# A decoder stack on one core: causal mask added and maximum taken by one VectorE instruction in self attention, softmax row tile by row tile, normalisations in a pipeline

## What is computed

```python
x = x + _L0_attn_ref(_layernorm(x), ...)    # causal self attention, 16 heads, 4 key heads
x = x + _L0_xattn_ref(_layernorm(x), ...)   # each token picks 2 of its 4 sets
x = x + _L0_ffn_ref(_layernorm(x), ...)     # 16 experts, 4 per token
x = x + _L1_attn_ref(_layernorm(x), ...)    # gated delta rule, 16 heads
x = x + _L1_xattn_ref(_layernorm(x), ...)   # queries: x; keys: x and 64 context tokens
x = x + _L1_ffn_ref(_layernorm(x), ...)     # 128 experts, 48 kept, 8 per token
```

```python
def _layernorm(x, axis=-1, eps=1e-05):
    m = jnp.mean(x, axis=axis, keepdims=True)
    v = jnp.var(x, axis=axis, keepdims=True)
    return (x - m) / jnp.sqrt(v + eps)
...
    scores = jnp.einsum('bkgqd,bksd->bkgqs', qg, k) * scale
    causal = jnp.triu(jnp.full((S, S), -jnp.inf, dtype=x.dtype), k=1)
    scores = scores + causal
    attn = jax.nn.softmax(scores, axis=-1)
    out = jnp.einsum('bkgqs,bksd->bkgqd', attn, v)
```

## Time and profile before

| | us |
|---|---|
| median of 3 runs (4146.95 to 4150.4) | 4150.28 |
| the profiled execution | 4138.86 |
| its span, first to last instruction | 4137.1 |
| PE, DVE, ACT, POOL busy in it | 3579.5, 2639.7, 1644.6, 1412.7 |
| rotation of the keys on VectorE, start to end: self, cross | 0.74, 1.19 |
| `at_wo`'s transfer is issued; TensorE's first projection starts | 7.24; 27.20 |
| self attention, about | 26 to 675 |
| delta rule, about | 1151 to 2889 |
| cross attention, about | 2943 to 3870 |

### The profile page before, as it was taken

The page is one execution under the profiler, slowest core; times in us unless marked ns, Lnnn a source line. Parts: engine busy times, 40 slices in busy tenths (PEclk is TensorE's granted clock), DMA queues, the critical chain, the costliest instruction groups (busy, mean ns, idle before and its releaser), DMA issues. The chain is left out here.

```text
span 4137.1 us, 57933 instructions
## 1 busy us (share of the span) xinstructions
PE 3579.5 (87%) x17616; PEld 2756.4 (67%) x17616; DVE 2639.7 (64%) x7558; ACT 1644.6 (40%) x4218; POOL 1412.7 (34%) x2085
## 2 busy tenths in 40 slices
PE   7999997589678999999999999998499999999565
PEld 5676765445366888888888888886356556556454
DVE  5666565532247888888888888873666666666531
ACT  3444442133234455555554545441243443443221
POOL 0000000068615555555555555552111111111055
PEclk9999998589868999999999999999699999999665
DMA  2000002335500111111111111110100000000346
GB/s 75 0 0 0 0 0 68 116 65 85 117 14 19 40 28 40 29 36 30 35 37 27 37 27 39 28 21 12 57 1 0 0 0 0 0 0 0 115 111 144
DMA packets 220951, 149.99 MB, mean 36 GB/s; under 512 B 117104, under 2 KB 208656, under 8 KB 220208
## 3 DMA queue, kind: packets, MB, share of 16 engines
q1 hardware_dynamic: 193664, 111.49, 10.5%
q0 software_dynamic: 22848, 31.69, 4.6%
q10 hardware_dynamic: 4224, 4.19, 0.3%
HBM read 105.64 MB, written 41.61 MB: 36 GB/s over the span
## 5 line engine op out<-in xcount | busy, mean ns | idle before, releaser
L1921 DVE SCALAR_TENSOR_TENSOR dl_y<-ps,dl_taps,dl_y 128x255 f32<-128x255 f32 (+2 forms) x1536 | 652.4, 474 | 129.5 <-ACT dl_y L1817 125.3
L1652 PE MATMUL ps<-xnT,dl_wkqv 128*128 128x256 f32 x2048 | 546.2, 393 | 27.5 <-DVE dl_lp L1964 21.8
L1652 PEld LDWEIGHTS ps<-xnT,dl_wkqv 128*128 128x128 f32 x2048 | 370.7, 194 | 78.3 <-issue 34.9
L379 POOL TENSOR_TENSOR at_rs<-at_ss,mhalf 128x15 f32<-128x15 f32 x32 | 125.5, 3922 | 745.1 <-DVE at_ss L566 745.1
L1575 POOL TENSOR_TENSOR dl_rn<-dl_n,mhalf 128x4 f32<-128x4 f32 x128 | 173.4, 1354 | 548.0 <-DVE dl_n L1937 548.0
L465 PE MATMUL ps<-at_shared,at_v 128*128 128x256 f32 (+2 forms) x1280 | 315.7, 380 | 4.6
L1817 ACT ACTIVATE dl_y<-ps,dl_taps 128x256 f32<-128x256 f32 x512 | 260.2, 560 | 106.1 <-PE ps L1652 106.0
L405 PE MATMUL ps<-at_wq,at_xb 128*128 (+1 forms) x512 | 247.6, 618 | 36.0 <-POOL at_xb L373 33.9
L441 PE MATMUL ps<-at_kT,at_qT 128*128 128x320 f32 (+2 forms) x1024 | 271.2, 397 | 2.8 <-ACT at_kT L671 2.8
L1593 POOL TENSOR_TENSOR dl_inv_u<-dl_inv_u,dl_inv_tmp 64x30 f32<-64x30 f32 (+14 forms) x480 | 260.1, 542 | 37.6
L465 PEld LDWEIGHTS ps<-at_shared,at_v 128*128 128x128 f32 (+1 forms) x1280 | 211.1, 190 | 89.3 <-issue 64.0
(11 more groups left out here) (348 smaller groups left out, 7798.5 us busy)
## 6 DMA issues: line engine op xcount, KB each, us to landing
dl_grow<-decay_rows SPq DMA_DIRECT2D x128, 128.0 KB, 3.0
sp_wgu<-in_w1gu SPq DMA_DIRECT2D x12, 768.0 KB, 5.3
dl_wkqv<-in_w1kqv SPq DMA_DIRECT2D x16, 512.0 KB, 4.6
delta_diag<-dl_lp SPq DMA_DIRECT2D x512, 8.0 KB
dl_diag<-delta_diag_tt SPq DMA_DIRECT2D x512, 8.0 KB, 1.7
moe_wgu<-in_w0gu SPq DMA_DIRECT2D x16, 448.0 KB, 10.6
sp_wd<-in_w1d SPq DMA_DIRECT2D x12, 384.0 KB, 6.2
dl_wo<-in_w1o SPq DMA_DIRECT2D x16, 256.0 KB, 3.6
```

The costliest lines, as they stand in the source:

```text
L1652: last = nc.tensor.matmul(bank(h, m // 2, (m % 2) * S, (m % 2 + 1) * S), wkqv[h][:, c, m * P:(m + 1) * P], k.xnT[:, c, u.seq * S:(u.seq + ...
L1921: last = nc.vector.scalar_tensor_tensor(y[h][:, m, back:S], bank(h, m // 2, (m % 2) * S, (m % 2 + 1) * S - back), taps[h][:, m, KC - 1 - b ...
```

## The change

1. **Mask.** In self attention the product with the identity is gone. VectorE's `tensor_tensor_reduce` reads a score tile in PSUM and a mask in SBUF, writes their sum to the probabilities' buffer and gives its row maximum; it shows as two rows named ISA, the second reading the accumulator. ScalarE's exponential then reads SBUF. The mask is loaded once as 128x256 float32 instead of two 128x128 bf16 tables.
2. **Row tiles.** In both attentions every hand-over in the softmax counts tiles: one maximum, one negated maximum, one reciprocal per tile, and one semaphore step each.
3. **Order.** VectorE's list for two rows is the new function `softmax`. The copy `keep_probs` of the first row stands in it before the scaling of the second row's second tile, and the rotation of the keys stands behind the whole of it.
4. **Power.** The root-mean-square power on GpSimd is two instructions, over 64x1 and 128x10 elements, instead of one over 128x15.
5. **Normalisation.** VectorE takes the statistics of turn i + 1 before it normalises turn i; it normalises two tiles of four and ScalarE the other two (as scale times x plus shift); the transposes are in two halves with a semaphore each; the transposed result alternates between two PSUM halves, and ScalarE copies turn i - 1 after its part of turn i.

```diff
@@ layernorm, VectorE
-            for i in range(turns):
+            def stats(i):
...
+            def normalise(i):
+                n, b = i + base, i % 2
+                if n >= 1:
+                    dve.wait_ge(k.ln_normed_a, n)
+                    dve.wait_ge(k.ln_turned_d, n)
+                dve.wait_ge(k.ln_pow, n + 1)
+                nc.vector.scalar_tensor_tensor(k.ln_nmr[b][:, HQ:Q], k.ln_mv[b][:, HQ:Q, 0], -1.0, k.ln_rstd[b][:, HQ:Q],
+                                               ALU.mult, ALU.mult).then_inc(k.ln_shift, 1)
+                for q in range(HQ):
...
+            stats(0)
+            for i in range(turns):
+                if i + 1 < turns:
+                    stats(i + 1)
+                normalise(i)
@@ layernorm, ScalarE
             for i in range(turns):
-                act.wait_ge(k.ln_turned, i + base + 2)
-                nc.scalar.copy(k.xnT[:, :, i * Q * P:(i + 1) * Q * P], k.ps[0][:, 0:DC, :]).then_inc(k.ln_stored, 1)
+                n, b = i + base, i % 2
+                if n >= 1:
+                    act.wait_ge(k.ln_turned_a, n)
...
+                act.wait_ge(k.ln_shift, n + 1)
+                for q in range(HQ, Q):
+                    last = nc.scalar.activation(xn(i, q), k.x[:, i * Q + q, :], ACT.Identity,
+                                                bias=k.ln_nmr[b][:, q:q + 1], scale=k.ln_rstd[b][:, q:q + 1])
+                last.then_inc(k.ln_normed_a, 1)
+                if i >= 1:
+                    keep(i - 1)
+            keep(turns - 1)
@@ attention, GpSimd
-                    nc.gpsimd.tensor_tensor(rs[h][:, :, :], ss[h][:, :, :],
-                                            k.mhalf[:, 0:KT * (G + 1)].rearrange("p (t g) -> p t g", t=KT), ALU.pow)\
+                    nc.gpsimd.tensor_tensor(rs[h][0:CTX, TB, G:G + 1], ss[h][0:CTX, TB, G:G + 1], k.mhalf[0:CTX, 0:1], ALU.pow)
+                    nc.gpsimd.tensor_tensor(rs[h][:, 0:TB, :], ss[h][:, 0:TB, :],
+                                            k.mhalf[:, 0:TB * (G + 1)].rearrange("p (t g) -> p t g", t=TB), ALU.pow)\
@@ attention, TensorE, score
-                        last = nc.tensor.matmul(o[:, 0:nk], qT[h][:, r, t * P:(t + 1) * P],
-                                                kT[h][:, 0:nk], start=True, stop=cross)
-                        if not cross:
-
-                            last = nc.tensor.matmul(o[:, t * P:nk], k.identb[:, :],
-                                                    k.causb[:, :], start=False, stop=True)
-                    last.then_inc(s.scored[h], 1)
+                        nc.tensor.matmul(o[:, 0:nk], qT[h][:, r, t * P:(t + 1) * P],
+                                         kT[h][:, 0:nk], start=True, stop=True).then_inc(s.scored[h], 1)
@@ attention, TensorE, turn_probs
+                    pe.wait_ge(s.probs_ready[h], u * (G * TB) + (r * TB + 1))
+                    for j in range(2 if cross else 1):
+                        turn(j, 0)
+                    pe.wait_ge(s.probs_ready[h], u * (G * TB) + (r * TB + 2))
+                    for j in range(2):
+                        last = turn(j, 1)
+                    if cross:
+                        for t in range(TB):
+                            last = turn(2, t)
                     last.then_inc(s.probs_turned[h], 1)
@@ attention, VectorE, row_max in self attention
+                        dve.sem_inc(s.masking[h], 1)
+                        link(h, u, f"max{r}{t}",
+                             nc.vector.tensor_tensor_reduce(probs[h][:, m, 0:nk], k.ps[h][:, m, 0:nk], k.causal[:, S - nk:S],
+                                                            1.0, NEG, ALU.add, ALU.max, mx[h][:, m:m + 1]))
+                        ins_ = nc.vector.tensor_scalar(nb[h][:, m:m + 1], mx[h][:, m:m + 1], -scale, None, ALU.mult)
+                    ins_.then_inc(s.max_ready[h], 1)
@@ attention, VectorE, order
+                def softmax(h, u, r):
+                    row_max(h, u, r, 0)
+                    row_max(h, u, r, 1)
+                    row_max(h, u, r + 1, 0)
+                    norm_probs(h, u, r, 0)
+                    row_max(h, u, r + 1, 1)
+                    norm_probs(h, u, r, 1)
+                    norm_probs(h, u, r + 1, 0)
+                    keep_probs(h, u, r)
+                    norm_probs(h, u, r + 1, 1)
...
                     if back is not None:
-                        row_max(g, back, 0)
-                        row_max(g, back, 1)
-                        norm_probs(g, back, 0)
-                        norm_probs(g, back, 1)
-                        keep_probs(g, back, 0)
+                        softmax(g, back, 0)
                         keep_probs(g, back, 1)
...
-                        row_max(g, back, 2)
-                        row_max(g, back, 3)
-                        norm_probs(g, back, 2)
+                        softmax(g, back, 2)
                     if front is not None:
                         rotate(h, front, TB)
                     if back is not None:
-                        norm_probs(g, back, 3)
-                        keep_probs(g, back, 2)
                         keep_probs(g, back, 3)
@@ attention, ScalarE, exps
-                    act.wait_ge(s.max_ready[h], u * G + (r + 1))
                     for t in range(TB):
+                        act.wait_ge(s.max_ready[h], u * (G * TB) + (r * TB + t + 1))
...
-                        last = nc.scalar.activation(probs[h][:, m, 0:nk], k.ps[h][:, m, 0:nk], ACT.Exp,
+                        source = k.ps[h][:, m, 0:nk] if cross else probs[h][:, m, 0:nk]
+                        last = nc.scalar.activation(probs[h][:, m, 0:nk], source, ACT.Exp,
                                                     bias=nb[h][:, m:m + 1], scale=sc, accum_out=den[h][:, m:m + 1])
-                    last.then_inc(s.exp_done[h], 1)
+                        last.then_inc(s.exp_done[h], 1)
```

136 lines of the change are left out of this document (72 added, 64 removed).

## The result

| | before | after |
|---|---|---|
| median of 4 runs, us | 4149.6 | 4234.1 |
| lowest, highest | 4147.0, 4150.4 | 4230.3, 4239.5 |
| profiled execution: time, span | 4138.9, 4137.1 | 4230.5, 4228.7 |
| 30 self-attention stages (all but the first), first score to first score | 593.0 (19.77 each) | 640.5 (21.35 each) |
| 31 cross-attention stages | 874.7 (28.22 each) | 948.9 (30.61 each) |

The change makes the kernel slower: ratio 1.021, 95% interval 1.0196 to 1.0224. The forecast was 4178 us: the sign was right, the size was not. Between the two profiled executions the span grows by 91.6 us: 47.5 in self attention (forecast 29.5), 74.2 in cross attention (forecast 29.5), and -30.1 in the rest, where -30.8 was forecast. So the whole error lies in the two attentions. (The medians differ by 84.5 us.)

What follows compares the result with a forecast made beforehand. Both attentions were taken as nearly TensorE-bound, each normalisation turn as one chain. Self attention +29.5, cross attention +29.5, first and last half stages +1, normalisations -31.8 gave +28 on 4150.3: 4178 us, range 4146 to 4215.

Steps and rivals of the forecast that it cites:

- The hand-over in self attention: Self attention: TensorE and VectorE wait for each other around row 0's copy; stage 19.77 to 20.72 us, +29.5 us in all.
- VectorE's tile step: Self-attention softmax: masked maximum, negated maximum and gaps per tile, priced at 0.49 and 0.62 us.
- The late keys in cross attention: Cross attention: later keys' rotation delays squares and ScalarE's copy of row 3; +0.95 us a stage, +29.5 us in all.
- The masked maximum: Self attention, VectorE: 0.34 and 0.47 us for 128 and 256 columns, bounds 0.28 and 0.41 to 0.47 and 0.74.
- rival 1: Self attention: masked maximum runs at half rate, 0.47 and 0.74 us; +54 us instead of 29.5, total 4203; chance 14%.
- The power: Cross attention, GpSimd: 2.9 us for both instructions instead of 3.92, bounds 2.6 and 3.9; gains nothing by itself.
- The normalisations: Five normalisations go from 21.2 to 15.3 us, -29.5 in all; the first gains 2.3; sum -31.8 us.
- rival 4: Cross attention: TensorE's clock falls behind its new waits, 1.7 us lost a stage, 53 us in all, total 4231; chance 4%.
- The stretch of the earlier trace: Last half stage of self attention, TensorE waiting for scalings: granted clock 0.66 over 5 us, 1.7 us lost.

Runs made afterwards that it cites:

- experiment 1: Changed kernel with VectorE's copy of a row's turned probabilities put behind the next row's last scaling, in both attentions: 4166.6 us, 1.0066 of the kernel before.
- experiment 9: Changed kernel with GpSimd's copy of the next tokens in self attention made to wait until the halves are summed: 4234.7 us, one run.
- experiment 7: Changed kernel with masks back on TensorE as products, plain maximum and exponential from PSUM, tiles and order as changed: 4237.4 us, 1.022 of the kernel before.
- experiment 10: Changed kernel with unused products filling TensorE's waits in both attentions, and GpSimd's two powers made one over 15 columns: 4199.1 us, one run.
- experiment 5: Kernel before with only the new normalisation and its buffers, attention as before: 4112.8 us, 0.9938 of the kernel before.
- experiment 3: Changed kernel with three unused TensorE products between mix of row 2 and mix of row 3 in cross attention: 4194.0 us, 1.0142 of the kernel before.
- experiment 4: As experiment 3, plus one unused product between the two tiles' transposes of rows 2 and 3 in self attention: 4188.6 us, one run.
- experiment 6: Kernel before with only the mask moved to VectorE's masked maximum, mask products removed, exponential from SBUF, whole rows: 4165.5 us, 1.0052 of the kernel before.
- experiment 8: Kernel before with only the rotation of the keys moved behind row 3's scalings and row 2's copy, both attentions: 4214.0 us, 1.0178 of the kernel before.
- keys_early: As experiment 1, with the rotation of the keys also put ahead of row 3's last scaling: 4112.9 us, 0.9941 of the kernel before.

## Why the prediction was right and where it failed

- **The hand-over in self attention.** Forecast 20.72 us a stage with a wait of 0.7 in row 1; measured 20.92 and 21.13 at the full clock with 0.73. The cause holds: without it the stage is 19.63 (experiment 1). Two things are lacking. The slow scaling gives 0.37 more in every second stage: with it gone these take 20.76 (experiment 9), so that the stages are 20.8 on average, 0.1 above the forecast. And VectorE's tile step, from one masked maximum to the next, is 0.59 and 0.72 us (296.26, 296.85 and 297.57; forecast 0.49 and 0.62), since 0.25 to 0.27 passes between the negated maximum and the next masked one, where I took 0.11. Ahead of each masked maximum the code increments a semaphore; in experiment 7, with neither the increment nor the masked instruction, 0.09 to 0.10 passes. Which of the two takes the time was not tried.
- **The late keys in cross attention.** Forecast 28.24 + 0.95 = 29.19; measured 29.31 in stages without a dip. ScalarE's copy of row 3 came 19.3 us into the stage, as worked out.
- **The masked maximum.** 0.28 and 0.42 us, at the lower bound; rival 1 (half rate) is out. The Trainium skill (Vector Engine (DVE) Microarchitecture Reference, "Points that are easy to get wrong") states its halved rate for the scalar-tensor-tensor shape with two SBUF sources; with one source in PSUM these rows grow by 0.14 us over 128 columns, as the L536 rows do, so there is no half rate here. No run has both sources in SBUF.
- **The power.** Forecast 2.9 us for both, measured 1.73 + 1.96 = 3.69. A price per column was wrong: ten columns take only 0.23 us longer than one, yet fifteen take 3.92, twice as long as ten, and why stays open. The 0.8 us too little did not matter, since the chain ends with `give` all the same; with the old power a stage without dips is 0.25 longer (experiment 10; forecast 0.5). So the split is worth 7.5 us in cross attention against the old power in the new order (one run of each kernel).
- **The normalisations.** Forecast -31.8, measured -31.7 between the spans and -27 by the medians (experiment 5). Each of the five takes 15.8 us from its first statistics to the end of its last copy, where 15.3 was forecast, and 21.2 before.
- **The step that failed is the clock: the sum kept TensorE at its full clock in all steady stages, and rival 4, which did not, got too little weight.** I had the mechanism, the place (behind the waits ahead of `mix` of row 3 and `give`), a price of 1.7 us a stage and a time of 4231, and gave it 4%, with the reason "The steady stages wait up to 1.1 us at 1.00". It came true in 29 of 31 cross stages at 1.40 us each: 40.7 us by experiment 3, and 10 more in self attention by experiment 4, where the forecast had none. The reason given was the mistake: it looked at the longest single wait. What is different in the changed kernel is how much idle time stands together: ahead of `mix` of row 3 and of `give` 1.42 and 0.56 us, 2.3 us apart (3378.05 and 3380.37), where before 1.10 stood ahead of row 3's transposes and 0.56 ahead of `give`, 4.6 us apart. That this nearness decides was not tried by itself; that the wait of 1.42 us is needed for the dips, experiment 3 shows. The stretch of the earlier trace rows, which the prediction cited and set aside, has waits nearer still to each other, and the `mix` behind them takes 2.77 us, where it takes 1.56 at the full clock:

```profile
659.73 0.55 PE L455 MATMUL ps<-ident,at_probs 128*128 128x128 f32 x3 [1.77 <-DVE at_probs L600]
660.62 0.90 PE L455 MATMUL ps<-ident,at_probs 128*128 128x128 f32 x3 [0.34 <-DVE at_probs L600]
```

The forecast's 28, 41 and 10 for the dips, 8 for self stages longer by 0.28 (21.00 in experiment 4; about 5 of the 8 are the slow scaling) and 4 for cross stages longer by 0.12 make 91 of the 91.6 us. The price was a little high, 1.7 us against 1.4. The forecast range reached 4215, so this rival lay outside it from the start.

What stays open: which pattern of waits just suffices. Experiments 1, 6 and 8 have stages with the same waits to a few hundredths, some with a dip and some without; the last half stage of the kernel before has waits of 1.77 and 0.33 us again, 8 us behind those above, and no dip follows; and in keys_early a single 1.24 us wait brings none in cross attention while 0.71 and 0.86 us bring 14 in self attention.

## What to carry to other kernels

When an edit leaves TensorE waiting more often within one stage of a loop, price the clock as well as the wait. Look at all its idle time there, and not at the longest wait alone, and look for a stretch of the present kernel where it idles as much; here the last half stage of self attention was that stretch and was set aside. Taking products off an engine that then waits is no gain, and can be a loss (experiment 6), while unused products in a wait can be one (experiment 3). Look also at what an engine that is through sooner sets off on a third one: here GpSimd's copy fell on a scaling and doubled it (experiment 6). On an in-order engine, put the instruction that waits for another engine behind the one that this engine is waiting for: two moved calls took a cross stage from 29.31 to 27.46 us at the full clock.

## What the runs showed of the hardware

- TensorE's granted clock falls to 1.2 GHz for 3.4 us (in some stages of experiments 1 and 8 for 6.8) behind waits that are each under 1.8 us (0.75, 1.42 and 0.56 in the changed kernel), and this repeats at the same place of a loop, 29 times in 31. Filling one wait of 1.4 us with unused products ended it.
- GpSimd's power takes 1.73 us for 64x1 elements, 1.96 for 128x10 and 3.92 for 128x15.
- A VectorE scaling from SBUF to SBUF takes 0.71 us instead of 0.29 while GpSimd copies in SBUF for 0.61 (306.42 and 306.44); with the copy moved it takes 0.29. The same holds for all 14 slow scalings of the changed kernel, and for 28 scalings of 256 columns in experiment 7 (0.56 to 0.71 instead of 0.35). The Trainium skill (SBUF — State Buffer, "SBUF: two separate sides") says that GpSimd and a VectorE instruction in a 2-port mode share a pair of ports, which one of them holds for its whole instruction while the other blocks. By that the scaling ends a little behind 306.44 + 0.61 = 307.05; it ended at 307.13, and in experiment 7 the scalings of 256 columns end 0.15 behind the copy, so the ends agree. The starts don't settle it: the scaling's row stands 0.02 us ahead of the copy's. No row shows the mode, but this scaling takes only 0.07 us longer for 256 columns than for 128 (0.28 and 0.35), where the L536 rows take 0.13.
- The addition of the mask with a maximum, PSUM and SBUF to SBUF, takes 0.28 and 0.42 us for 128 and 256 columns, about as long as the product of PSUM and SBUF in the earlier trace rows (0.28 and 0.41).
